# The steps of five hand-written engine programs in another order, in a kernel of gated attention and a spiking feed-forward part

## The reference, cut to what matters

```python
def _mlstm_cell(q, k, v, igate_w, igate_b, fgate_w, fgate_b, ln_scale):
    ifg = jnp.concatenate([q, k, v], axis=-1)
    ig = (ifg @ igate_w.T + igate_b).T
    fg = (ifg @ fgate_w.T + fgate_b).T
    ...
    cs = jnp.cumsum(jax.nn.log_sigmoid(fg), axis=1)
    log_D = where(tril, cs[:, :, None] - cs[:, None, :], -inf) + ig[:, None, :]
    max_log_D = jnp.max(log_D, axis=-1, keepdims=True)
    D_mat = jnp.exp(log_D - max_log_D)
    C = (jnp.einsum('hsd,htd->hst', qh, kh) / np.sqrt(DH)) * D_mat
    normalizer = jnp.maximum(jnp.abs(C.sum(axis=-1, keepdims=True)), jnp.exp(-max_log_D))
    h = jnp.einsum('hst,htd->hsd', C / (normalizer + EPS), vh)
    ...
    return layernorm(h) * ln_scale

def _L0_ffn_ref(x, W_fc, W_proj):          # W_fc 1024x256, W_proj 256x1024
    h = jnp.square(jax.nn.relu(x @ W_fc.T))
    y = h @ W_proj.T
    # 5 steps: mem = 0.9 * mem + y - reset; a spike where mem > 1; the mean of the spikes
    ...

x = x + tanh(g_xattn) * cell(layernorm(x), ctx, ctx, ...)
x = x + tanh(g_ffn) * ffn(layernorm(x), W_fc, W_proj)
```

## Time and profile before

| what | value |
|---|---|
| three runs | 615.34, 616.83, 615.02 us |
| profiled execution: span (no other time of its own is recorded) | 615.3 us |
| PE busy | 571.4 us, 93% |
| DVE, ACT, POOL busy | 526.3, 485.8, 493.3 us (86, 79, 80%) |
| PE weight loads (PEld) busy | 479.2 us |
| DMA | 71.34 MB, mean 116 GB/s |
| granted TensorE clock, whole span | 0.98 |

### The profile page before, as it was taken

The page is one execution under the profiler, slowest core; times in us unless marked ns, Lnnn a source line. Parts: engine busy times, 40 slices in busy tenths (PEclk is TensorE's granted clock), DMA queues, the critical chain, the costliest instruction groups (busy, mean ns, idle before and its releaser), DMA issues.

```text
span 615.3 us, 17747 instructions
## 1 busy us (share of the span) xinstructions
PE 571.4 (93%) x6032; PEld 479.2 (78%) x6032; DVE 526.3 (86%) x1291; ACT 485.8 (79%) x1011; POOL 493.3 (80%) x541
## 2 busy tenths in 40 slices
PE   0568988999999999999999999999999999999995
PEld 0357888887888888888788888888888888887894
DVE  4789889989989898989989898989999888878446
ACT  3776878897888888888888788888888777776673
POOL 4878889996997889887997889887997887955542
PEclk9995989999999999999999999999999999999998
DMA  8775736664664637662663637752675427401002
GB/s 271 168 145 115 160 74 124 168 139 95 124 149 96 155 84 127 171 146 70 123 163 83 158 83 131 187 126 70 121 167 130 87 48 148 121 4 35 0 2 70
DMA packets 73193, 71.34 MB, mean 116 GB/s; under 512 B 8720, under 2 KB 68752, under 8 KB 73104
## 3 DMA queue, kind: packets, MB, share of 16 engines
q1 hardware_dynamic: 71888, 70.00, 50.5%
q10 hardware_dynamic: 1216, 0.21, 0.2%
HBM read 27.44 MB, written 8.39 MB: 58 GB/s over the span
## 4 chain that ended last, share of the span: by engine, by line
PE 82%; SPq 7%; DMA 3%; ACT 2%; issue 2%; DVE 2%; POOL 1%; ACTq 0%; POOLq 0%; DVEq 0%
PE z_ps L1069 28%; PE y_ps L1135 26%; PE qk_ps L773 4%; PE arg_ps L758 4%; PE misc_ps L503 4%; SPq L706 3%; PE misc_ps L569 2%; SPq L553 2%; PE pv_ps L822 2%; PE pv_ps L820 2%; PE pv_ps L821 2%; PE pv_ps L897 2%; DMA x<-w_proj_t 2%; PE y_ps L1164 1%; PE arg_ps L1135 1%
## 5 line engine op out<-in xcount | busy, mean ns | idle before, releaser
L802 POOL TENSOR_TENSOR c_lo<-decay 128x512 bf16<-128x512 f32 x128 | 132.7, 1043 | 31.9 <-DVE decay L792 31.8
L1112 POOL TENSOR_TENSOR sq_lo<-w_raw,sq_hi 128x512 fp32r<-128x512 f32 (+1 forms) x96 | 111.8, 1166 | 39.6 <-ACT w_raw L1092 39.3
L1069 PE MATMUL z_ps<-x_hi,wfc_hi 128*128 128x512 f32 (+1 forms) x288 | 114.4, 397 | 1.8 <-ACT w_raw L1079 1.8
L1069 PE MATMUL z_ps<-x_hi,wfc_lo 128*128 128x512 f32 (+1 forms) x288 | 106.1, 368 | 0.0
L1069 PE MATMUL z_ps<-x_lo,wfc_hi 128*128 128x512 f32 (+1 forms) x288 | 105.9, 368 | 0.0
L1135 PE MATMUL y_ps<-sq_hi,wpr_hi 128*128 128x512 f32 (+1 forms) x256 | 103.8, 406 | 0.0
L1135 PE MATMUL y_ps<-sq_hi,wpr_lo 128*128 128x512 f32 (+1 forms) x256 | 97.4, 380 | 0.0
L1135 PE MATMUL y_ps<-sq_lo,wpr_hi 128*128 128x512 f32 (+1 forms) x256 | 97.1, 379 | 0.0
L792 DVE TENSOR_TENSOR decay<-qk_ps,decay 128x512 f32<-128x512 f32 x128 | 87.0, 680 | 9.4 <-ACT decay L784 6.5
L784 ACT ACTIVATE decay<-arg_ps,lqk_col 128x512 f32<-128x512 f32 x128 | 86.6, 677 | 10.5 <-PE arg_ps L761 9.5
L1153 DVE SCALAR_TENSOR_TENSOR spikes<-y_ps,spikes 128x1024 bf16<-128x1024 f32 (+1 forms) x64 | 73.8, 1153 | 1.2
(11 more groups left out here) (193 smaller groups left out, 1727.8 us busy)
## 6 DMA issues: line engine op xcount, KB each, us to landing
x_in<-x SPq DMA_DIRECT2D x32, 256.0 KB, 3.2
kT_in<-ctx_cols SPq DMA_DIRECT2D x32, 256.0 KB, 3.2
v_in<-ctx_rows SPq DMA_DIRECT2D x32, 256.0 KB, 4.3
k_stack<-kT_hi SPq DMA_DIRECT2D x64, 128.0 KB, 3.2
k_stack<-kT_lo SPq DMA_DIRECT2D x64, 128.0 KB, 3.7
q_stack<-qT_hi SPq DMA_DIRECT2D x64, 128.0 KB, 4.1
q_stack<-qT_lo SPq DMA_DIRECT2D x64, 128.0 KB, 4.3
out<-w_raw SPq DMA_DIRECT2D x32, 256.0 KB, 3.4
```

The costliest lines, as they stand in the source:

```text
L802: e.tensor_tensor(c_lo[i % NCH][:, :], c, top(c), ALU.subtract).then_inc(sem("c_lo"), 1)
L1069: ins = e.matmul(z_ps[:, tokens(q)], lhsT, rhs, start=(n == 0), stop=(n == len(terms) - 1))
L1112: e.tensor_tensor(sq_lo[n % NSQ][:, tokens(q)], relu[n % NRE][:, tokens(q)], sq_hi[n % NSQ][:, tokens(q)].bitcast(fp32), ALU.subtract).the ...
```

## The change

All five programs, and `MISC_ORDER` with them, are written in another order. Each engine still does exactly the steps that it did: 210 on SP, 706 on ACT, 579 on DVE, 806 on PE and 519 on POOL. No step function, buffer or wait is different (one wait follows `MISC_ORDER`: whose turn is next). A step stands on average 2.0 places from where it was on SP, 0.9 on ACT, 0.5 on DVE, 0.6 on PE and 2.2 on POOL; the farthest is moved 13. The loops `for n in range(1, 6)` are written out, and their five turns no longer have one order. Lines move by 3 up to the programs (line 376 is 379 after, 1135 is 1138). The programs stand at 1191, 1404, 2112, 2693 and 3501 now.

```diff
-            order = [("q", 0), ("g", 0), ("q", 1), ("gT", 0), ("q", 2), ("g", 1), ("fT", 0), ("gT", 1), ("q", 3),
...
+            return [("q", 0), ("g", 0), ("q", 1), ("gT", 0), ("g", 1), ("q", 2), ("fT", 0), ("q", 3), ("gT", 1),
...
         def sync_program(e):
             load_x(e, 0)
             load_x(e, 1)
+            load_x(e, 2)
+            load_x(e, 3)
             load_k(e, 0)
+            load_k(e, 1)
+            load_values(e, 0)
+            load_values(e, 1)
             setup_load_wfc(e)
...
         def scalar_program(e):
             setup_load_g(e)
+            setup_tanh(e)
             setup_load_gates(e)
-            setup_tanh(e)
             ln1_rstd(e, 0)
+            setup_load_scale(e)
+            ln1_apply(e, 0)
+            ln1_apply(e, 1)
+            q_hi(e, 0)
             split_wfc_hi(e, 0)
-            ln1_apply(e, 0)
-            q_hi(e, 0)
-            ln1_apply(e, 1)
...
         def gpsimd_program(e):
-            setup_pool(e)
-            setup_own(e)
             setup_fixed(e)
             k_hi(e, 0)
+            k_hi(e, 1)
+            setup_pool(e)
             k_lo(e, 0)
+            setup_own(e)
+            k_hi(e, 2)
+            k_lo(e, 1)
+            k_lo(e, 2)
```

The relu step came right behind the split, and now comes right ahead of it. In the PE program, the same kind of swap stands near the end:

```diff
             z_step(e, 17, 6)
+            y_step(e, 17, 3)
             count_T(e, 15)
-            y_step(e, 17, 3)
             z_step(e, 17, 7)
```

More of the change, by code:

```diff
@@ L1205, in sync_program @@
             load_a_rows(e, 0)
+            stack_heads(e, 1)
             load_k(e, 4)
             load_k(e, 5)
[L1208 removed]
             load_values(e, 2)
+            load_values(e, 3)
             load_a_rows(e, 1)
@@ new lines, in scalar_program @@
+            decay_exp(e, 9, 0)
+            ln3_rstd(e, 7)
+            ln1_apply(e, 13)
+            decay_exp(e, 9, 1)
+            relu_step(e, 3, 6)
+            gates_out(e, 12)
+            decay_exp(e, 9, 2)
+            q_hi(e, 13)
+            ln2_rstd(e, 8)
+            ln3_apply(e, 7)
+            square(e, 3, 6)
+            decay_exp(e, 9, 3)
+            relu_step(e, 3, 7)
+            square(e, 3, 7)
+            gates_out(e, 13)
+            x2_hi_step(e, 7)
+            ln3_rstd(e, 8)
@@ new lines, in scalar_program @@
+            decay_exp(e, 14, 1)
+            ln1_rstd(e, 9)
+            relu_step(e, 6, 0)
+            square(e, 6, 0)
+            relu_step(e, 6, 1)
+            ln1_apply(e, 18)
+            decay_exp(e, 14, 2)
+            relu_step(e, 6, 2)
+            square(e, 6, 1)
+            ln1_apply(e, 19)
+            square(e, 6, 2)
+            relu_step(e, 6, 3)
+            q_hi(e, 18)
+            ln2_rstd(e, 13)
+            decay_exp(e, 14, 3)
+            relu_step(e, 6, 4)
+            gates_out(e, 18)
@@ new lines, in scalar_program @@
+            square(e, 8, 0)
+            relu_step(e, 8, 1)
+            ln1_apply(e, 22)
+            decay_exp(e, 18, 2)
+            relu_step(e, 8, 2)
+            q_hi(e, 22)
+            square(e, 8, 1)
+            square(e, 8, 2)
+            relu_step(e, 8, 3)
+            decay_exp(e, 18, 3)
+            ln1_apply(e, 23)
+            ln2_rstd(e, 17)
+            relu_step(e, 8, 4)
+            gates_out(e, 22)
+            square(e, 8, 3)
+            square(e, 8, 4)
+            decay_exp(e, 19, 0)
@@ new lines, in scalar_program @@
+            square(e, 9, 3)
+            relu_step(e, 9, 4)
+            ln2_rstd(e, 19)
+            decay_exp(e, 20, 3)
+            q_hi(e, 24)
+            square(e, 9, 4)
+            relu_step(e, 9, 5)
+            decay_exp(e, 21, 0)
+            ln3_rstd(e, 19)
+            square(e, 9, 5)
+            ln1_apply(e, 25)
+            decay_exp(e, 21, 1)
+            relu_step(e, 9, 6)
+            gates_out(e, 24)
+            ln3_apply(e, 19)
+            q_hi(e, 25)
+            ln2_rstd(e, 20)
@@ new lines, in scalar_program @@
+            q_hi(e, 30)
+            square(e, 12, 1)
+            square(e, 12, 2)
+            relu_step(e, 12, 3)
+            ln1_apply(e, 31)
+            decay_exp(e, 26, 3)
+            ln2_rstd(e, 25)
+            relu_step(e, 12, 4)
+            decay_exp(e, 27, 0)
+            gates_out(e, 30)
+            square(e, 12, 3)
+            square(e, 12, 4)
+            relu_step(e, 12, 5)
+            ln3_rstd(e, 25)
+            q_hi(e, 31)
+            gates_out(e, 31)
+            square(e, 12, 5)
```

2487 lines of the change are left out of this document (1845 added, 642 removed), and 13 rows, old and new, of the table SLOTS.

## The result

The changed kernel takes 623.31 us (median of 4 runs, 621.49 to 624.53), the kernel before 615.18 beside it (4 runs, 615.02 to 616.83). So the kernel is slower by 7 us (ratio) to 8 us (medians), where 4.5 us less were forecast. In the four later series of runs the kernel before had medians of 617.06 to 617.42; the changed kernel was timed in the first series alone, so kernels of different series are compared by their ratios and traces.

A forecast was written before the change was run, and what follows sets the result against it. PE was taken as the bound, busy 571.4 of 615.3 us, with its waits at the ends. Terms −2.8 − 0.5 − 1.0 − 0.7 + 0 + 0.5 = −4.5 gave 610.8 us, range 605.5 to 614.6.

The forecast's parts named there:

- 140 to 600 us ... I take 0: Middle, PE computing 459.48 of 460.00 us: nothing to gain, a loss possible, priced at 0.
- The fourth rival: Middle: late POOL splits ahead of `state_lo` stall PE, 2.7 us a turn over five turns, 624 us; chance 0.10.
- Its sign: Any PE idle time over 2 us between 140 and 600 us, released by POOL, would show the forecast wrong.
- The start, −2.8: Up to the first `arg`, at 33.25 us before: gain between 1.8 and 3.8 us, taken as −2.8.
- the early end: First transpose: loads land 2.8 us earlier, `ident` ready at 11.3 us, a gain of 4.6 us.
- the gate weights: Start: their early loads from ACT's queue might hold x and keys up; issuing them later would land all 2.8 us earlier.
- the late end: First transpose: second keys land at 11.9 us, `ident` ready only at 14.1, a gain of 1.8 us.
- −0.5 from 30 to 62: 30 to 62 us: moved transposes and products fill PE waits; −0.5 us, between 0 and −1.6.
- −1.0 at 84: 84 us: relu ahead of ACT's split saves PE's wait and half clock there; −1.0 us, between 0 and −3.2.
- −0.7 from 90 to 122: 90 to 122 us: loads moved earlier in SP's queue, gain bounded by 2.29 us of PE idle; −0.7 us.
- The rule quoted from the Trainium skill: 84 us: clocks are lost in longer idle gaps, so only the wait could go and the sum be about 1 us higher.
- The tail, +0.5: After 600 us: `count_T(15)` behind a y step delays DVE's `out_step(15)`; loss of 0.5 us, between 0 and 0.8.

The follow-up runs named there:

- kernel 2: Kernel before with only the middle of all five programs, about 125 to 556 us, in the changed kernel's order; 622.36 us, ratio 1.0070.
- 8: Kernel before with one swap on ACT, relu_step(1, 0) ahead of am_split(3, 0); 615.99 us, ratio 0.9991.
- 9: Kernel before with load_x(27) moved four places down SP's queue, behind load_k(27); 619.58 us, ratio 1.0035.
- kernel 4: Kernel before with SP's queue alone in the new order from its 50th to its 206th step; 628.32 us, ratio 1.0189.
- kernel 7: Kernel before with only the very start, up to about 35 us, in the new order on all five engines; 614.79 us, ratio 0.9968.
- 3: Changed kernel with SP's queue alone in the old order from its 50th to its 206th step; 641.89 us, ratio 1.0386.
- 11: Kernel before with the new order up to 35 us and relu_step(1, 0) ahead of am_split(3, 0) on ACT; 613.62 us, ratio 0.9956.

## Why the prediction was wrong

The forecast was 610.8 and the time 623.31, outside the range on the slow side. Step by step:

- **"140 to 600 us ... I take 0."** This is the step that failed. The middle lost 7.5 us (457.4 to 464.9; with the old front 8.1, kernel 2). I read full use of PE as "it can only lose" and then priced the loss at nothing, though every one of the turns had been reordered and PE had no idle time to hide a late step in.
- **The fourth rival** had the sign and the place right and got 0.10. Its mechanism was too narrow, and that its full price, 624, lies next to the measured 623.31 is luck: it was five turns of 2.7 us with half clock in them, and the granted clock was 1.00 from 140 to 600 us. Its sign, over 2 us of idle time with POOL as releaser, did not come either; POOL ended 0.3 us of PE's waits there. I looked for a POOL split ahead of `state_lo`; the two largest losses came from SP's queue, one through a load of x that landed after DVE's list had reached its statistics, one through a row load. In the kernel before, x of 27 had landed 1.31 us ahead of its use, and x of the odd samples from 17 on between 0.65 and 1.42 us ahead of theirs. That could have been read beforehand, and set against a stack of 6.4 us that the new list puts in front. I had counted SP's moves as 2.0 places on average and looked at them only up to 122 us. The single places were cheaper than its 2.7 us, and there were more of them: about 168 us 1.0 was lost, from 193 to 196 0.7, at 216 0.6 and from 394 to 402 2.0; the other 3.2 of the 7.5 lie in pieces of about half a microsecond and less.
- **The start, −2.8.** The size of the early end was right, `ident` at 10.9, and the reason given for it, the gate weights, is not borne out: x of sample 1 landed at 9.27 in the profile of before and at 5.95 after, but in the four other traces with the old start it landed at 5.8 to 6.3 with the gate weights ahead of it all the same. What would have made the late end did not come either: the gate weights, issued at 5.08 in the changed kernel, landed only at 14.19, and the second keys at 8.75, well ahead of them. What delays three of those four (2, 8 and 9) is a step that I had passed over, `split_wfc_hi(0)` ahead of `ln1_apply(0)` on ACT: in kernel 2 the offsets were ready at 10.08, and ACT waited for the weights, which landed at 11.93, and split them first, as the timeline of ACT in kernel 2 below shows. (In kernel 4 the weights landed at 9.48, and there the offset was late.) The profiled pair gives 4.2 at the first `arg`, the mean over all traces 2.4. Of that, 1.8 is left at arg(7, 0) (mean 133.5 over the five old fronts, 131.6 over the six kernels that have the whole new one and its middle).

```profile
11.95 1.06 ACT L352 ACTIVATE wfc_hi<-w_raw 128x1024 fp32r<-128x1024 f32 x1 [4.10 <-DMA w_raw<-w_fc_t]
12.91 1.43 ACT L460 ACTIVATE xln<-x_in,off,rstd 128x256 f32<-128x256 f32 x2
```

- **−0.5 from 30 to 62, −1.0 at 84, −0.7 from 90 to 122.** Nothing of these 2.2 us can be seen. The six kernels with the whole new front come to arg(7, 0) at 131.6 on the mean, the two with the new start alone at 131.6 as well. The 1.7 us of clock were put down to the wait at 84 us; with the same wait the clock was 1.00 from 84 to 92 us in kernels 2, 7 and 9 and fell in kernel 4 and in the kernel before. The rule quoted from the Trainium skill (TensorE: Matmul & The Clock Gate, section HAM oscillation) spoke against giving them to this wait, and the runs agree with it so far: the wait of 1.47 us in kernel 2 has no half clock behind it. What took the clock in the others they do not show.
- **The tail, +0.5:** measured +0.4 (22.8 to 23.2, in each of the kernels with either tail).

Put together, −1.8 + 7.5 + 0.4 is +6.1 us, or 1.010, inside the interval of the measurement.

## What to carry to other kernels

Where hand-written in-order programs keep one engine full, a step can have a window of place only a few us wide: later, and an engine waits for it (x of 27, put behind four steps, cost 2.0 us); earlier, and it holds its own queue up (x of 31, 4.4 us too early, cost 6.1). Before such lists are reordered, take from the trace how far ahead of its use each load lands, and look first at loads with about 1.5 us or less to spare (x of 27 had 1.31) that the new order puts behind a long step. A reordering of a full stretch should be given a loss and not a zero, and the whole list of one engine should not be exchanged alone (kernels 3 and 4 lost 19 and 15 us by it).

## What was not expected

Identical orders scatter in the front and hardly behind it. The five traces with the old start have the first `arg` at 29.3, 31.6, 32.3, 32.5 and 33.3 us, the nine with the new one within 0.9 us of each other. They scatter again up to arg(7, 0), and the two do not go together: a first `arg` at 29.31 and one at 31.56 led to 131.88 and 131.80. From arg(7, 0) on, kernels 8 and 11 take the 457.4 us of the kernel before, and kernel 7 differs by its one wait. The trace of the kernel before was thus 1.5 us later than the mean of its like at the first `arg`, and a part of the gain that I forecast was read from it.
